# Experts that read routed rows in place, with a second product in four row tiles

## The chip, the cores and the metric

The kernel runs on one core of a Trainium2 chip. The metric is the device time of one execution in microseconds (us), the median of several runs.

## The reference, cut to what matters

The block has two halves: a gated causal cross attention (16 blocks of 128 rows, 256 wide, 16 heads), and a mixture of 32 experts, each with 4 sets. The second half is what the change works on:

```python
grouped = x.reshape(B, g, t, d)                      # groups of t = 32 rows
logits = jnp.einsum('bgtd,des->bgtes', grouped, controller) + tie
perm = (logits == jnp.max(logits, axis=-3, keepdims=True)).astype(x.dtype)
dispatched = jnp.einsum('bgtd,bgtes->bgesd', grouped, perm)
inner = jax.nn.relu(jnp.einsum('bgesd,desf->bgesf', dispatched, f1) + bias)
intermediate = jnp.einsum('bgesf,esfd->bgesd', inner, f2)
out = jnp.einsum('bgesd,bgtes->bgtd', intermediate, perm)
```

In each of 64 groups every (expert, set) slot, 128 in all, picks one row of 32; the row goes through a small network (256 to 32, relu, 32 to 256) and is added back to the row it came from.

## The kernel before, in words

Everything is float32; E = 256 is held as KH = 2 halves of 128 on the partitions. The engines run separate programs joined by semaphores; their order is written out by hand, with loops (`Fori`) whose bodies are unrolled by 2, 4 or 8. The names: PE multiplies matrices, DVE and ACT are the vector and the scalar engine, POOL is the third elementwise engine, SP issues loads and stores in the order of its program.

The start: SP issues the context tiles `cT` of blocks 0 and 1, the rows `xs`, the controller `ctrl_sb` (L211), then RING = 8 blocks of expert weights `wx` (L213, 256.5 KB each: both matrices and the bias), then in a loop the further context tiles (L220). ACT turns each context tile into its high part in `context_high` (L660), for block 2 right after the first four exponentials of block 0 (L688, L694).

Attention runs block by block over four chunks of four heads (`scores`, `weigh_v`, `transpose_p`, `softmax`, `attend`), then routing (`route`, L504 on PE): logits, a one-hot choice `pc` of a row for each slot, its transpose, and a product (L528) that gives the chosen rows. ACT (L670), for the last two blocks DVE too (L1031), keeps them in `routed[P, KH, GROUPS, SLOTS]`, one copy of 128x512 for each half of a block.

The experts: for each expert DVE first copies its four slots of all 64 groups from `routed` to a packed tile `xe` (L1038, `stage`, three experts ahead). PE multiplies `f1` of each set by it (`expert_in`, L548: 8 matmuls in four column tiles of 32, one for each set, out to a bank). DVE adds the bias and takes relu set by set (`hidden`, L1052: four instructions of 32x64) into the diagonal blocks of `hb`, whose other blocks POOL zeroed at the start. PE multiplies `f2` by this block-diagonal tile (`expert_out`, L556: 2 matmuls of full depth 128 with 256 moving columns). ACT writes the result back over the same slots of `routed` (L765). `expert_in` of the next expert stands ahead of `expert_out` of this one. SP loads expert e + 8 once expert e is through (L226).

The last stage, for each of 16 blocks: DVE packs four groups from `routed` into `yg` (L1074), PE transposes them (`transpose_y`, L596, 8 transposes), ACT copies the result to `ys` (L775, two copies), POOL copies the block's choice `permT` to `pg` (L313), PE multiplies both (`combine`, L611, four column tiles), DVE adds it to `xs` (L1078) and SP stores it (L231). The transposes of block b + 1 stand ahead of `combine` of block b.

In the trace each f32 matmul is two instructions, each with its own weight load; a transpose is one.

Of the kernel before, what the change touches and what calls it, by code (L numbers as in the profile page):

```python
# [17 lines left out]
F32 = mybir.dt.float32  # L18
# [7 lines left out]
P = 128  # L26
# [14 lines left out]
RING = 8  # L41
XR = 4
# [7 lines left out]
def build(nc, x, ctxT, wattn, gbo, ctrl, wexp, constf, out):  # L50
    with ExitStack() as ctx:
# [6 lines left out]
        bank = [ctx.enter_context(nc.psum_tensor(f"bank{i}", [P, 512], F32)) for i in range(8)]  # L58
# [18 lines left out]
        tg = sb("tg", [P, 2])  # L77
        ctrl_sb = sb("ctrl_sb", [P, KH, SLOTS])
# [32 lines left out]
        routed = sb("routed", [P, KH, GROUPS, SLOTS])  # L111
        wx = sb("wx", [P, RING, KH * P + E + 1])
        xe = sb("xe", [P, XR, KH, NS, GROUPS])
        hb = sb("hb", [P, 2, NS, GROUPS])
        yg = sb("yg", [P, 2, KH, NG, SLOTS])
        pg = sb("pg", [P, 2, P])
# [6 lines left out]
        small_loaded = sem("small_loaded")  # L123
        gates_loaded = sem("gates_loaded")
# [57 lines left out]
        xe_ready = sem("xe_ready")  # L182
        h_done = sem("h_done")
        h_ready = sem("h_ready")
        e_done = sem("e_done")
        e_kept = sem("e_kept")

        permT_kept = sem("permT_kept")
        yg_ready = sem("yg_ready")
        pg_ready = sem("pg_ready")  # L190
# [13 lines left out]
        def _(sp):  # L204
# [6 lines left out]
            sp.dma_start(ctrl_sb[:, :, :], ctrl).then_inc(small_loaded, 16)  # L211
# [9 lines left out]
            with sp.Fori(1, NE // RING) as i:  # L221
                e = i * RING
                for r in range(RING):

                    sp.wait_ge(e_done, e + (r - RING + 1))
                    sp.dma_start(wx[:, r], wexp[e + r]).then_inc(wx_loaded[r], 16)  # L226
# [10 lines left out]
        def _(pool):  # L237
            pool.memset(qz[:, :, :, :, :], 0.0).then_inc(zeroed, 1)
            pool.memset(va[:, :, :, :], 0.0).then_inc(zeroed, 1)
            pool.memset(hb[:, :, :, :], 0.0).then_inc(zeroed, 1)  # L240
# [30 lines left out]
            for k in range(2):  # L271
                split_context(k, k + 1)
            pool.wait_ge(bo_ready, 1)
# [30 lines left out]

            pool.wait_ge(permT_kept, NB)
            for k in range(2):
                pool.tensor_copy(pg[:, k, :], permT[:, k, :]).then_inc(pg_ready, 1)
            with pool.Fori(1, NB // 2) as i:
                b = i * 2
                for k in range(2):  # L310

                    pool.wait_ge(c_done, b + (k - 1))
                    pool.tensor_copy(pg[:, k, :], permT[:, b + k, :]).then_inc(pg_ready, 1)  # L313
# [3 lines left out]
        def _(pe):  # L317
# [76 lines left out]
            def attend(b, k, first=False, second=False, third=False, final=False):  # L394


                for c in range(NC):
# [45 lines left out]
                    if final and c == 3:  # L443
                        pe.wait_ge(small_loaded, 16)
# [97 lines left out]
            BH, BE = bank[0:2], bank[2:4]  # L542

            def expert_in(r):
                k = r % 2
                for s in range(NS):
                    for h in range(KH):
                        last = pe.matmul(BH[k][s * F:(s + 1) * F, 0:GROUPS],  # L548
                                         wx[:, r, h * P + s * F:h * P + (s + 1) * F], xe[:, r % XR, h, s, :],
                                         start=(h == 0), stop=(h == KH - 1), tile_position=(0, s * F))  # L550
                last.then_inc(h_done, 1)

            def expert_out(r):
                k = r % 2
                for h in range(KH):
                    last = pe.matmul(BE[k][:, h * E:(h + 1) * E], wx[:, r, KH * P + h * P:KH * P + (h + 1) * P],  # L556
                                     hb[:, k].rearrange("p s g -> p (s g)"), start=True, stop=True)
                last.then_inc(e_done, 1)

            def expert(e, r, loads):  # L560

                if loads is not None:
                    pe.wait_ge(wx_loaded[(r + 1) % RING], loads)
                    pe.wait_ge(xe_ready, e + 2)
                    if r > 0 or not isinstance(e, int):

                        pe.wait_ge(h_ready, e)
                    expert_in((r + 1) % RING)
                pe.wait_ge(h_ready, e + 1)
                if not isinstance(e, int) or e >= 2:  # L570

                    pe.wait_ge(e_kept, e - 1)
                expert_out(r)
# [4 lines left out]
            pe.wait_ge(wx_loaded[0], 16)  # L578
            pe.wait_ge(xe_ready, 1)
            expert_in(0)  # L580
            for e in range(2):
                expert(e, e, 16)
            with pe.Fori(0, NE // RING - 1) as i:
                for r in range(2, RING + 2):
                    expert(i * RING + r, r % RING, i * 16 + 16 * (1 + (r + 1) // RING))
            for r in range(2, RING):
                expert(NE - RING + r, r, 16 * (NE // RING) if r < RING - 1 else None)
# [4 lines left out]
            def transpose_y(k):  # L592
# [6 lines left out]
            def combine(b, k, early=False, final=False):  # L599

                if not final:
                    pe.wait_ge(yg_ready, b + 2)
                    if not isinstance(b, int) or b >= 1:
                        pe.wait_ge(ys_ready, b)
                    transpose_y(1 - k)
                pe.wait_ge(ys_ready, b + 1)
                pe.wait_ge(pg_ready, b + 1)
                if not early:
                    pe.wait_ge(yo_ready, b - 1)
                for g in range(NG):  # L610
                    last = pe.matmul(BC[k][g * T:(g + 1) * T, 0:E], pg[:, k, g * T:(g + 1) * T],  # L611
# [3 lines left out]
            pe.wait_ge(e_kept, NE)  # L615
            pe.wait_ge(yg_ready, 1)
            transpose_y(0)
            combine(0, 0, early=True)
            combine(1, 1, early=True)
            with pe.Fori(1, (NB - 2) // 2) as i:  # L620
                b = i * 2
                for k in range(2):
                    combine(b + k, k)
            combine(NB - 2, 0)
            combine(NB - 1, 1, final=True)
# [3 lines left out]
        def _(act):  # L629
# [37 lines left out]
            def keep_d(b, k, halves=KH):  # L667
                act.wait_ge(d_done, b + 1)
                for h in range(halves):
                    last = act.activation(routed[:, h, bass.ds(b * NG, NG), :],  # L670
                                          bank[5 - 2 * k + h][:, :].rearrange("p (g s) -> p g s", g=NG), ACT.Copy)
# [89 lines left out]
            with act.Fori(0, NE // 2) as i:  # L761
                e = i * 2
                for k in range(2):
                    act.wait_ge(e_done, e + (k + 1))
                    act.activation(routed[:, :, :, bass.ds((e + k) * NS, NS)],  # L765
                                   bank[2 + k][:, :].rearrange("p (h s g) -> p h g s", h=KH, s=NS), ACT.Copy)\
                        .then_inc(e_kept, 1)


            with act.Fori(0, NB // 2) as i:  # L770
                b = i * 2
# [378 lines left out]
```

## Time and profile before

| what | value |
|---|---|
| median of 3 runs | 329.9 us (329.48 to 330.55) |
| profiled execution, first to last instruction | 326.0 us |
| PE busy | 286.1 us (88%) |
| DVE busy | 264.4 us (81%) |
| ACT busy | 196.3 us (60%) |
| POOL busy | 112.3 us (34%) |
| PE granted clock over the span | 0.990 of full |

A time of an instruction group is given in us, a mean duration in ns. PEld is PE's weight load, which overlaps its matmuls. An engine's busy share says how full it is, not whether the end waits for it.

### The profile page before, as it was taken

How to read it: one execution, taken by the hardware profiler on the slowest of the kernel's cores; microseconds unless marked ns; L12 is line 12 of the kernel's file. 1: busy time of each engine (PE TensorE's matmuls, PEld its weight loads, DVE VectorE, ACT ScalarE, POOL GpSimd, SP SyncE). 2: the span in 40 equal slices, each digit the busy share in tenths (PEclk: the TensorE clock that was granted, in tenths of full speed). 3: DMA queues.
4: the chain of work that ended last, by engine and by line, in shares of the span. 5: the costliest groups of instructions: out<-in, count | busy, mean ns of one | idle time of the engine just before them, and what ended most of it. 6: DMA issues, size and time to landing. Idle time of an engine off the chain costs nothing.

```text
span 326.0 us, 9319 instructions
## 1 busy us (share of the span) xinstructions
PE 286.1 (88%) x3088; PEld 209.9 (64%) x3088; DVE 264.4 (81%) x675; ACT 196.3 (60%) x738; POOL 112.3 (34%) x156
## 2 busy tenths in 40 slices
PE   2299899999999999999999968899687777787995
PEld 2247577777787778787877647677365444555662
DVE  1968988978787878787879868999899999985663
ACT  2057777777777777777777863687232233225663
POOL 4124554455445644563455561455000000000110
PEclk9999999999999999999999997999899999999999
DMA  7940000000000000000000000000045454300222
GB/s 208 369 182 4 18 18 0 19 18 17 0 16 16 16 0 16 16 16 0 16 0 0 2 2 0 1 2 0 0 131 135 151 136 129 97 2 16 80 80 82
DMA packets 12355, 16.41 MB, mean 50 GB/s; under 512 B 1200, under 2 KB 7728, under 8 KB 12336
## 3 DMA queue, kind: packets, MB, share of 16 engines
q1 hardware_dynamic: 11472, 14.83, 14.9%
q10 hardware_dynamic: 864, 1.33, 1.3%
q8 instruction: 11, 0.18, 0.3%
q14 instruction: 8, 0.07, 0.1%
HBM read 14.06 MB, written 2.10 MB: 50 GB/s over the span
## 4 chain that ended last, share of the span: by engine, by line
PE 57%; DVE 26%; issue 11%; DMA 2%; ACT 2%; POOL 1%; DVEq 0%; ACTq 0%; SPq 0%; POOLq 0%
PE bank L359 10%; PE bank L352 9%; PE bank L368 9%; DVE hb L1052 8%; PE bank L328 8%; PE bank L338 7%; PE bank L596 5%; PE bank L348 3%; PE bank L611 3%; DVE xe L1038 2%; DMA xs<-in_x_dram 2%; DVE nmax L912 2%; PE bank L528 1%; DVE permb L901 1%; DVE stats L824 1%
## 5 line engine op out<-in xcount | busy, mean ns | idle before, releaser
L688 ACT ACTIVATE pr<-bank,nmax 128x128 f32<-128x128 f32 x256 | 90.3, 368 | 25.1 <-PE bank L359 18.5
L263 POOL TENSOR_TENSOR pr<-pr,rsum 128x512 f32<-128x512 f32 x64 | 66.6, 1040 | 89.4 <-DVE rsum L861 89.1
L352 PE MATMUL bank<-kd,qz 128*32 128x128 f32 (+3 forms) x512 | 66.7, 437 | 0.0
L368 PE MATMUL bank<-pT,va 128*32 128x128 f32 x512 | 62.3, 274 | 1.7 <-ACT pT L653 1.3
L912 DVE TENSOR_REDUCE nmax<-bank 128x4 f32<-128x512 f32 x64 | 44.0, 687 | 19.9 <-PE bank L352 18.6
L688 ACT ACTIVATION_READ_ACCUMULATOR pr<-bank,nmax 128x1 f32 x256 | 52.9, 207 | 0.0
L368 PEld LDWEIGHTS bank<-pT,va 128*32 128x32 f32 x512 | 38.6, 110 | 17.1 <-ACT pT L653 2.5
L556 PE MATMUL bank<-hb,wx 128*128 128x256 f32 x128 | 37.5, 417 | 12.5 <-DVE hb L1052 12.5
L765 ACT ACTIVATE routed<-bank 128x512 f32 x32 | 19.1, 597 | 45.0 <-PE bank L556 45.0
L359 PE MATMUL bank<-cf,pr 128*128 128x128 f32 x256 | 42.0, 286 | 1.6 <-POOL pr L263 1.5
L1052 DVE TENSOR_SCALAR hb<-bank,wx 32x64 f32<-32x64 f32 x128 | 36.0, 281 | 2.9 <-PE bank L548 0.6
L359 PEld LDWEIGHTS bank<-cf,pr 128*128 128x128 f32 x256 | 26.8, 140 | 15.1 <-issue 11.5
L556 PEld LDWEIGHTS bank<-hb,wx 128*128 128x128 f32 x128 | 22.4, 195 | 19.6 <-DVE hb L1052 15.9
L313 POOL COPY pg<-permT 128x128 f32 x14 | 4.1, 294 | 87.5 <-PE bank L611 87.5
L653 ACT ACTIVATE pT<-bank 128x512 f32<-128x512 f32 x32 | 19.1, 598 | 18.0 <-PE bank L359 18.0
L328 PE MATMUL bank<-cT,w 128*128 128x128 f32 x128 | 18.1, 286 | 6.2 <-DMA w<-in_wattn_dram 5.6
L874 DVE COPY pT<-bank 128x512 f32<-128x512 f32 x32 | 22.1, 689 | 1.7
L843 DVE TENSOR_SCALAR xn<-xs,mv,rs 128x256 f32 (+1 forms) x32 | 23.4, 732 | 0.0
L1038 DVE COPY xe<-routed 128x512 f32 (+1 forms) x32 | 22.4, 710 | 1.0
L775 ACT ACTIVATE ys<-bank 128x512 f32<-128x512 f32 x32 | 17.3, 596 | 9.4 <-PE bank L596 9.4
L670 ACT ACTIVATE routed<-bank 128x512 f32 (+1 forms) x30 | 16.4, 595 | 8.9 <-PE bank L528 8.7
L848 DVE TENSOR_TENSOR kd<-bank,cf 128x512 f32<-128x512 f32 x32 | 21.4, 672 | 0.4 <-PE bank L328 0.4
(91 smaller groups left out, 538.8 us busy)
## 6 DMA issues: line engine op xcount, KB each, us to landing
wx<-in_wexp_dram SPq DMA_DIRECT2D x32, 256.5 KB, 2.7
cT<-in_ctxT_dram SPq DMA_DIRECT2D x16, 128.0 KB, 2.0
xs<-in_x_dram SPq DMA_DIRECT2D x4, 512.0 KB, 10.3
out_dram<-xs SPq DMA_DIRECT2D x16, 128.0 KB, 1.7
w<-in_wattn_dram ACTq DMA_DIRECT2D x4, 256.0 KB, 7.7
cf<-in_constf_dram ACTq DMA_DIRECT2D x1, 148.0 KB, 5.9
gb<-in_gbo_dram ACTq DMA_DIRECT2D x1, 129.0 KB, 7.6
ctrl_sb<-in_ctrl_dram SPq DMA_DIRECT2D x1, 128.0 KB, 10.7
```

The lines of the kernel that those rows point to most:

```text
L263: pool.tensor_tensor(pr[:, c % 2], pr[:, c % 2], rsum[:, c * HC:(c + 1) * HC, None].to_broadcast([P, HC, P]), ALU.mult)\
L328: last = pe.matmul(dst[:, o * P:(o + 1) * P], weight[:, i, o * P:(o + 1) * P], src[:, i, :], start=(i == 0), stop=(i == KH - 1))
L338: last = pe.matmul(dst[:, 0:E], stationary, moving, start=(q == 0), stop=(q == len(parts) - 1))
L352: last = pe.matmul(bs[r, :, 0:(j + 1) * DP], qz[:, k, c // 2, c % 2, r], kd[:, k, c // 2, :, 0:(j + 1) * DP], start=False, stop=True, tile ...
L359: last = pe.transpose(BT[:, j * P:(j + 1) * P], pr[:, c % 2, j, :], ident)
L368: last = pe.matmul(BO[k][j * DP:(j + 1) * DP, o:o + P], va[:, k, c * HC + j, D * (1 - odd):][:, 0:DP], pT[:, c % 2, j * P:(j + 1) * P], st ...
L556: last = pe.matmul(BE[k][:, h * E:(h + 1) * E], wx[:, r, KH * P + h * P:KH * P + (h + 1) * P], hb[:, k].rearrange("p s g -> p (s g)"), sta ...
L688: last = act.activation(pr[:, c % 2, j, :], BS[c % 2][:, j * P:(j + 1) * P], ACT.Exp, bias=nmax[:, c * HC + j:c * HC + j + 1], accum_out=p ...
L843: dve.tensor_scalar(xn[:, k, :], xs[:, b, :], mv[:, b, 0:1], rs[:, bass.ds(b, 1)], ALU.subtract, ALU.mult).then_inc(ready, 1)
L912: dve.tensor_reduce(nmax[:, c * HC:(c + 1) * HC], BS[c % 2][:, :].rearrange("p (j t) -> p j t", j=HC), AX_X, ALU.max, negate=True).then_in ...
L1038: dve.tensor_copy(xe[:, k].rearrange("p h s g -> p h g s"), routed[:, :, :, bass.ds(e * NS, NS)]).then_inc(xe_ready, 1)
L1052: last = dve.tensor_scalar(hb[q, k, s, :], bank[k][q, 0:GROUPS], wx[q, r, KH * P + E:], 0.0, ALU.add, ALU.max)
```

## The change: what it does

- `routed` is laid out as [P, KH, SLOTS, GROUPS], and slots are ordered set by set, so the 64 groups of one slot are contiguous. The controller is loaded into `ctrl_in` and POOL reorders its columns into `ctrl_sb`, after a wait for the load, ahead of its first `bias_x`. Routing's copies (ACT and DVE) write four groups (16 bytes) for each of 128 slots.
- `xe`, `yg`, `pg` and the zeroing of `hb` are gone. `expert_in` and the last stage's PE instructions read `routed` and `permT` directly; a transpose reads its 128 slots 256 bytes apart.
- One relu for each expert, 128x64: ACT does the even experts (with Relu and a bias column), DVE the odd ones. `hb` is [P, 4, GROUPS], and the first product of an expert goes to bank e % 4.
- The second product is made for a pair of experts: 16 matmuls, each for one expert, half and set, in row tile s (32 rows of weights, 128 columns, 64 moving columns), to bank 4 + s. ACT copies banks 4 and 5, DVE banks 6 and 7 back to `routed`.
- RING is 16. SP issues 16 expert blocks at the start, the other 16 as pairs are done.
- In the last stage ACT makes one copy over two banks for each block, and DVE only the sum.
- The experts and the last stage are written out without loops.

```diff
-RING = 8
+RING = 16
+HR = 4
+PAIRS = NE // 2
...
-            sp.dma_start(ctrl_sb[:, :, :], ctrl).then_inc(small_loaded, 16)
+            sp.dma_start(ctrl_in[:, :, :], ctrl).then_inc(small_loaded, 16)
...
+            for e in range(RING, NE):
...
+                sp.wait_ge(e_done, (e - RING) // 2 + 1)
+                sp.dma_start(wx[:, e - RING], wexp[e]).then_inc(wx_loaded[e - RING], 16)
...
+            pool.wait_ge(small_loaded, 16)
+            pool.tensor_copy(ctrl_sb[:, :, :].rearrange("p h (s e) -> p h s e", s=NS),
+                             ctrl_in[:, :, :].rearrange("p h (e s) -> p h s e", s=NS)).then_inc(ctrl_ready, 1)
...
+            def expert_in(e):
...
+                for h in range(KH):
+                    for s in range(NS):
+                        last = pe.matmul(bank[e % HR][s * F:(s + 1) * F, 0:GROUPS],
+                                         wx[:, e % RING, h * P + s * F:h * P + (s + 1) * F],
+                                         routed[:, h, s * NE + e, :], start=(h == 0), stop=(h == KH - 1),
+                                         tile_position=(0, s * F), skip_group_check=True)
+                last.then_inc(h_done, 1)
+
+            def expert_out(p):
+
+                pe.wait_ge(h_ready_act, p + 1)
+                pe.wait_ge(h_ready_dve, p + 1)
+                if p > 0:
+                    pe.wait_ge(y_kept_act, p)
+                    pe.wait_ge(y_kept_dve, p)
+                for e in (2 * p, 2 * p + 1):
                     for h in range(KH):
...
+                        for s in range(NS):
+                            o = h * 2 * GROUPS + (e % 2) * GROUPS
+                            last = pe.matmul(bank[4 + s][:, o:o + GROUPS],
+                                             wx[s * F:(s + 1) * F, e % RING, KH * P + h * P:KH * P + (h + 1) * P],
+                                             hb[s * F:(s + 1) * F, e % HR, :], start=True, stop=True,
+                                             tile_position=(s * F, 0), skip_group_check=True)
                 last.then_inc(e_done, 1)
...
+            for p in range(PAIRS):
+                if p < PAIRS - 1:
+                    expert_in(2 * p + 2)
+                    expert_in(2 * p + 3)
+                expert_out(p)
...
-                        last = pe.transpose(BY2[k][g // 2][:, o:o + P], yg[:, k, h, g, :], ident)
+                        last = pe.transpose(BY2[k][g // 2][:, o:o + P], routed[:, h, :, b * NG + g], ident)
...
+            def hidden(e):
+
+                act.wait_ge(h_done, e + 1)
+                if e >= HR:
+                    act.wait_ge(e_done, (e - HR) // 2 + 1)
+                act.activation(hb[:, e % HR, :], bank[e % HR][:, 0:GROUPS], ACT.Relu,
+                               bias=wx[:, e % RING, KH * P + E:]).then_inc(h_ready_act, 1)
+
+            def keep_y(p):
+                act.wait_ge(e_done, p + 1)
+                act.activation(by_set[:, 0:2, :, 2 * p * GROUPS:2 * (p + 1) * GROUPS],
+                               banks[:, 4:6, 0:4 * GROUPS].rearrange("p s (h x) -> p s h x", h=KH), ACT.Copy)\
+                    .then_inc(y_kept_act, 1)
```

## Rows read from the trace of the kernel before

**Rows 1.** The page: span, busy time of each engine, the instruction queue's packets.
```profile
span 326.0 us, 9319 instructions
...
PE 286.1 (88%) x3088; PEld 209.9 (64%) x3088; DVE 264.4 (81%) x675; ACT 196.3 (60%) x738; POOL 112.3 (34%) x156
...
q8 instruction: 11, 0.18, 0.3%
```

**Rows 2.** Window of the experts: stretch, length, busy us (x) of PE, PEld, DVE, ACT, POOL, clock, DMA.
```profile
240.00:284.00 44.00, 34.50 (x460) 22.05 (x452) 41.56 (x114) 13.73 (x23) 0.00 (x0) 1.00 0.48 137
```

**Rows 3.** Timeline of one expert's round: start, length, engine, line, operation.
```profile
248.68 1.17 DVE L1052 TENSOR_SCALAR hb<-bank,wx 32x64 f32<-32x64 f32 x4
...
249.04 0.45 PE L548 MATMUL bank<-xe,wx 128*32 128x64 f32 x16
...
249.88 0.71 DVE L1038 COPY xe<-routed 128x512 f32 x1
...
249.90 1.13 PE L556 MATMUL bank<-hb,wx 128*128 128x256 f32 x4 [0.41 <-DVE hb L1052]
250.62 1.17 DVE L1052 TENSOR_SCALAR hb<-bank,wx 32x64 f32<-32x64 f32 x4
...
251.16 0.60 ACT L765 ACTIVATE routed<-bank 128x512 f32 x1 [1.32 <-PE bank L556]
```

**Rows 4.** Timeline at the experts' two ends.
```profile
230.81 0.69 DVE L1031 COPY routed<-bank 128x512 f32<-128x512 f32 x1 [0.29 <-PE bank L528]
...
232.44 0.96 PE L548 MATMUL bank<-xe,wx 128*32 128x64 f32 x32 [1.67 <-DVE xe L1038]
...
296.35 0.41 PE L596 MATMUL bank<-cf,yg 128*128 128x128 f32 x2 [1.60 <-DVE yg L1074]
```

**Rows 5.** Timeline of one round of the last stage.
```profile
316.69 0.86 PEld L596 LDWEIGHTS bank<-cf,yg 128*128 128x128 f32 x8 [0.41 <-issue]
316.69 1.09 PE L596 MATMUL bank<-cf,yg 128*128 128x128 f32 x8
...
317.71 0.16 PEld L611 LDWEIGHTS bank<-ys,pg 128*32 128x32 f32 x8 [0.17 <-issue]
317.71 0.64 PE L611 MATMUL bank<-ys,pg 128*32 128x256 f32 x8
...
318.28 1.09 PE L596 MATMUL bank<-cf,yg 128*128 128x128 f32 x8
```

**Rows 6.** Line 548: durations of one instruction, min/median/max ns, first and last start.
```profile
L548 PE MATMUL bank<-xe,wx x512: 216/219/317, 232.4 to 292.0; 128*32 128x64 f32 x171
```

**Rows 7.** Windows around the change from routing to the experts.
```profile
232.00:234.00 2.00, 0.91 (x32) 0.65 (x32) 1.96 (x7) 0.00 (x0) 0.00 (x0) 1.00 0.00 0
234.00:236.00 2.00, 1.70 (x4) 1.06 (x4) 1.89 (x6) 0.00 (x0) 0.00 (x0) 0.62 0.00 0
236.00:238.00 2.00, 2.00 (x20) 1.47 (x20) 1.89 (x6) 0.60 (x1) 0.00 (x0) 0.53 0.24 27
```

**Rows 8.** The start: issues, POOL, ACT's context copy; landing of L213, L220, L211.
```profile
4.84 3.59 SPq L211 DMA_DIRECT2D ctrl_sb<-in_ctrl_dram  x1
...
13.18 0.35 SPq L220 DMA_DIRECT2D cT<-in_ctxT_dram  x1
...
16.23 0.75 POOL L255 TENSOR_TENSOR xs<-xs,gb 128x256 f32<-128x256 f32 x1 [6.45 <-DVE gb L964]
...
21.87 0.43 ACT L660 ACTIVATE cTh<-cT 128x256 fp32r<-128x256 f32 x1
...
L213 SPq DMA_DIRECT2D wx<-in_wexp_dram x8: 432/432/872, 8.5 to 12.3; - x8
...
DMA to landing us min/median/max: 7.7/8.4/8.6
...
DMA to landing us min/median/max: 1.9/2.0/8.1
...
DMA to landing us min/median/max: 10.7/10.7/10.7
```

More of the change, by code:

```diff
@@ L56, in sem @@
             return ctx.enter_context(nc.semaphore(name))
-        bank = [ctx.enter_context(nc.psum_tensor(f"bank{i}", [P, 512], F32)) for i in range(8)]
+        banks = ctx.enter_context(nc.psum_tensor("banks", [P, 8, 512], F32))
+        bank = [banks[:, i, :] for i in range(8)]
         cf = sb("cf", [P, P + HC + P + NG + DP])
@@ L303, in _ @@
                     split_rows(NB - 1, 3)
[L305 to L313, printed above, removed]
         @block.tensor
@@ L553, in expert_out @@
[L553 to L557, printed above, removed]
-                last.then_inc(e_done, 1)
[L560 to L573, printed above, removed]
+            def expert_in(e):
+                pe.wait_ge(wx_loaded[e % RING], 16 * (e // RING + 1))
+                if e >= HR:
+                    if e % 2 == 0:
+                        pe.wait_ge(h_ready_act, (e - HR) // 2 + 1)
+                    else:
+                        pe.wait_ge(h_ready_dve, (e - HR) // 2 + 1)
+                for h in range(KH):
[5 more added lines that the diff above has]
+                last.then_inc(h_done, 1)
@@ L576, in _ @@
             pe.wait_ge(d_kept, NB)
             pe.wait_ge(d_kept_dve, 2)
-            pe.wait_ge(wx_loaded[0], 16)
-            pe.wait_ge(xe_ready, 1)
-            expert_in(0)
             for e in range(2):
[L582 to L587, printed above, removed]
+                expert_in(e)
@@ L1041, in hidden @@
-            def hidden(e, r, loads, early=False, left=NE):
-                k = r % 2
-                if not early:
-                    dve.wait_ge(e_done, e - 1)
-                dve.wait_ge(wx_loaded[r], loads)
-                dve.wait_ge(h_done, e + 1)
-                for s in range(NS):
-                    q = slice(s * F, (s + 1) * F)
-                    last = dve.tensor_scalar(hb[q, k, s, :], bank[k][q, 0:GROUPS], wx[q, r, KH * P + E:],
-                                             0.0, ALU.add, ALU.max)
-                last.then_inc(h_ready, 1)
-                if left > XR - 1:
-                    stage(e + XR - 1, (r + XR - 1) % XR)
@@ L1073, in stage_y, with hidden @@
[L1073 to L1076 removed]
+            def hidden(e):
+                dve.wait_ge(h_done, e + 1)
+                if e >= HR:
+                    dve.wait_ge(e_done, (e - HR) // 2 + 1)
+                dve.tensor_scalar(hb[:, e % HR, :], bank[e % HR][:, 0:GROUPS], wx[:, e % RING, KH * P + E:],
+                                  0.0, ALU.add, ALU.max).then_inc(h_ready_dve, 1)
@@ new lines, in keep_y @@
+            def keep_y(p):
+                dve.wait_ge(e_done, p + 1)
+                dve.tensor_copy(by_set[:, 2:4, :, 2 * p * GROUPS:2 * (p + 1) * GROUPS],
+                                banks[:, 6:8, 0:4 * GROUPS].rearrange("p s (h x) -> p s h x", h=KH))\
+                    .then_inc(y_kept_dve, 1)
+            hidden(1)
+            for p in range(PAIRS):
+                if p < PAIRS - 1:
+                    hidden(2 * p + 3)
+                keep_y(p)
+            for b in range(NB):
@@ L1093, in _ @@
-            dve.wait_ge(yT_done, NB - 2)
-            stage_y(NB - 1, 1)
-            for b in range(NB - 4, NB):
-                finish(b, b % 2)
 def constants():
```

139 lines of the change are left out of this document (44 added, 95 removed).

## The prediction, made before the change was run

> **What bounds the kernel now.** I read the page first: span 326.0 us, PE busy 88% of it, DVE 81% [rows 1]. The busy times by stage come next [rows 2]: from 240 to 284 us the experts, where DVE is busy 41.56 of 44 us and PE only 34.50. Attention and routing stand before, the last stage behind. The change works on the experts and the last stage, so I read one expert in order of time [rows 3]. The four relu pieces take DVE from 248.68 to 249.85, the staging copy for a later expert follows at once until 250.59, and the next relu starts at 250.62: a round of 1.94 us, all of it DVE. PE's first product (16 instructions, 0.45 us) and second (1.13 us) fit inside, and the second waits 0.41 us for relu. ACT's copy of 0.60 us is hidden. So 32 experts cost about 62 us, and the whole stretch from PE's first expert matmul at 232.44 to the first transpose at 296.35 is 63.9 us [rows 4]. In the last stage a round is 1.59 us (316.69 to 318.28), PE busy in all of it: 8 transposes, then 8 combining instructions [rows 5].
>
> The profiled execution is 326.0 us long from first to last instruction; the median of the runs is 329.9, so 3.9 us lie around the span. I sum against 326.0 and add 3.9.
>
> **Entry to the experts.** The staging copies go, PE reads the routed rows where they lie. Routing's last results are there at 231.50, PE starts at 232.44, after a wait for the staged tile [rows 4]. About 0.85 us saved.
>
> **Relu and copies.** Each relu becomes one instruction of 128x64 instead of four of 32x64; four take 1.17 us, one 0.28, by columns and not by partitions. ACT does the even experts: its 128x512 takes 0.60 us, so 64 columns take less, I say 0.25. The results of a pair are four banks of 256 columns; ACT and DVE each copy 512 columns, 0.60 us (the ACT row) and 0.69 us (the DVE copy from PSUM) [rows 3, 4]. Per pair DVE has 0.97 us and ACT 0.85, instead of twice 1.88 and twice 0.60. Neither bounds.
>
> **Second product.** It becomes 16 matmuls per pair, each 32 rows deep, 128 weight columns, 64 moving columns; in the trace every f32 matmul is two instructions, so 32 with 32 weight loads. No row of this kernel has tiles by rows; tiles by columns it has. The first product runs 16 such instructions in 0.45 us of which 0.22 is one's own length [rows 3, 6]: (0.45 - 0.22)/15 = 15 ns from one to the next. The combine does 8 weight loads of 32 columns in 0.16 us, so loads of four tiles overlap too [rows 5]. A load of 128 columns is longer: the transposes do 8 such in 0.86 us, 0.11 us each, with PE's passes beside them at the same pace [rows 5]; I take 0.11 us. If the four row tiles work side by side, each has 8 loads and 8 matmuls per pair, the load the longer one: 7 x 0.11 + 0.22 = 0.99 us from the first start to the last end. Bounds: matmul-paced as in the first product, 31 x 0.015 + 0.22 = 0.69 us; with no overlap of loads, 31 x 0.11 + 0.22 = 3.63 us. I take 0.99, by the nearest rows, which are all of four tiles.
>
> **The round of a pair.** The four result banks are single, so the chain is: second product of p, copy of p, second product of p+1. After a product's last end, 249.90 + 1.13 = 251.03, ACT starts at 251.16, 0.13 us later; DVE's copy is 0.69; and PE follows a DVE result within 0.05 us (249.85 to 249.90) [rows 3]. Round: 0.99 + 0.13 + 0.69 + 0.05 = 1.86 us. The first products of the next pair, 2 x 0.45 us with their mode changes, lie beside the copy and its end (PE alone: 0.88 for the stream, 0.5 for the first products, and 0.16 for each of two changes of tile shape, as between the last load of a transpose, 317.55, and the first of a combine, 317.71: about 1.7 [rows 5]); they are the cover, and if they took longer than 0.87 us the excess would be paid 16 times. Relu of the next pair fits under the product. Start-up: two first products, one relu, 1.3 us. Sum: 1.3 + 16 x 1.86 = 31.1 us for the 63.9 of before: 32.8 saved.
>
> **The clock** was granted at 0.62 and 0.53 of full from 234 to 238 us, that is the lower level (1.2 GHz) for about 3.4 us, after PE had been busy for only 0.91 of the 2 us before [rows 7]. Then DVE bound and it cost little; now PE's weight loads would be in the chain. I add 1.0 us, with 0 and 2 as ends.
>
> **Last stage.** The transposes read routed with 256 bytes between elements instead of a packed copy; in a transpose this is the stationary operand, the one loaded as weights. The loads now take 0.86 us for 8 beside PE's 1.09 [rows 5]; that difference is all the cover there is. No row has a PE operand so read. The nearest are ACT's and DVE's strided copies: the expert copy to 16-byte pieces 0.60 us, the staging read of 16-byte pieces 0.71 against 0.69 for a plain copy [rows 3, 4]. I take no cost; the other end is a load of twice 0.11 us: 8 x 0.11 x 16 = 14.1 us. DVE's packing, POOL's copies and the register arithmetic of the loop are hidden now, so what goes there gains nothing, except the first packing, which the 63.9 us already hold. ACT's one copy of 1024 columns instead of two is hidden under PE. The round stays 1.59 us.
>
> The Trainium skill (Advanced Engine Details and Errata, Memory Cachelines) says SBUF is read in 16-byte lines and that an access pattern with each element in another line is penalized. The ACT and DVE rows don't show it, but they have four floats per line; by the page every one of the 128 transposes would load slower, which is the rival of 316 below.
>
> **The longer ring.** Sixteen instead of eight expert blocks are queued by SP before the context tile of block 2. In the trace the eight are issued from 8.5 us, land 7.7 us after the first issue and 8.6 after the last (12.3), so from 16.2 to 20.9 us, one every 0.67 us [rows 8]. The context tile, issued right behind them at 13.18, lands 8.1 us later, at 21.3, where later ones take 2.0: it stands behind them in the queue. ACT reads it at 21.87, just in time [rows 8]. With eight more it lands at 21.3 + 8 x 0.67 = 26.7, and ACT sits in the middle of its softmax: 4.8 us. Behind that wait are all the exponentials of block 0 and so everything. PE and DVE can work ahead by some half a microsecond that counts; PE then idles some 3 us and may get the half clock for a while, as after routing. Sum: +5.0 us, ends 3.5 and 7. The new reordering of the controller by POOL waits for a load that lands at 4.84 + 10.7 = 15.5 us (4.84 is its issue, 10.7 its time to landing [rows 8]); POOL's next work was at 16.23 [rows 8]: no cost, at most 0.5. Of the expert loads, the second sixteen need 16 x 0.67 = 10.7 us and have seven rounds of 1.86 before the first is due: hidden. Routing's results are now written in 16-byte pieces, as ACT does in the expert stage at the same 0.60 us: no cost.
>
> **Sum.** 326.0 - 0.85 - 32.8 + 1.0 + 5.0 = 298.4 us; with 3.9 around it, 302 us.
>
> **Rivals.**
> 1. Slower: weight loads of row tiles don't overlap. Round 3.63 + 0.87 = 4.50 us, 16 of them 72.0 instead of 29.8: 344 us. It decides from 0.08 us per load on: the 28 us saved are 1.75 per pair, and (0.99 + 1.75 - 0.22)/31 = 0.08. For it: a load of 128 columns is seen every 0.11 us at best [rows 5], and none in row tiles. Against: loads of column tiles overlap fully.
> 2. Still faster than before, but less: the strided weight load takes double (14.1 us, 316 us); or loads overlap in twos (31 x 0.055 + 0.22 = 1.93, +15 us, 317 us); or the unrolled code, about 128 PE instructions per pair, is fetched too slowly. The instruction queue brought 0.18 MB in 11 packets over the whole kernel [rows 1]; were one needed for every two pairs and each uncovered by some 1.8 us (a guess below the 2.0 us of a small load [rows 8]), eight would be 14 us. The expert stage before shows no such stall, but it loops.
> 3. Better: row tiles paced as the first product, 0.30 us less per pair, 297 us; or the context tile comes in time after all, 5 us less, also 297. Both: 293.
>
> The Trainium skill (TensorE: Matmul & The Clock Gate, Part 3) gives 3.07 times for four row tiles with 512 columns, for tiles side by side, and says weight loads overlap when the row group differs; that is the forecast's case, but no run here shows row tiles yet.
>
> **How the numbers follow.** Forecast 302 us, chance 0.57 (296 to 308 with the bounds of the clock and the stall). Rival 1 0.16, rival 2 0.19, rival 3 0.06; that ring and experts cancel near no change 0.02. The range 294 to 319 takes in rivals 2 and 3 and leaves rival 1 out. A measurement tells about 0.3%, 1 us. Faster 0.81, same 0.02, slower 0.17.
>
> **What would show it.** The experts stage 31 us from first matmul to first transpose, rounds of 1.86 us and PE waiting for the copies; 32 instructions of the second product in about 1 us; ACT idle some 4.8 us before its context copy near 27 us, released by the DMA; last-stage rounds of 1.59 us. Wrong if rounds exceed 2.3 us, if transposes start more than 0.12 us apart, or if ACT's wait is absent.

## The result, and the profile after

| | before | after |
|---|---|---|
| median of the runs | 329.69 us (327.87 to 330.55) | 320.15 us (317.53 to 322.06) |
| profiled execution, first to last instruction | 326.0 us | 318.2 us |
| PE granted clock over the span | 0.990 | 0.930 |

The ratio of after to before is 0.9714, 95% interval 0.9657 to 0.9771. The sign was right, the size was not: 302 us was forecast with a range up to 319, and 18 of the 28 us expected did not come. Before and after were timed side by side. Within one changed kernel a slower run is one with a lower mean clock (after: 317.53 us at 0.938, 322.06 us at 0.919). The page of the changed kernel answers [rows 1]; its last line is the granted clock in 40 slices of 8 us:

```profile
span 318.2 us, 9488 instructions
...
PE 286.0 (90%) x3472; PEld 223.0 (70%) x3472; DVE 212.5 (67%) x531; ACT 190.8 (60%) x722; POOL 107.8 (34%) x140
...
PEclk9999999999999999999999997799999755559999
```

DVE is no longer the fullest engine, as intended. The slice of 7 and the four of 5 from 247 us on are the experts. The two 7s from 191 us on lie in attention and routing, which the change leaves nearly alone; such a dip there comes and goes from one profiled execution to the next. Next the windows there (stretch, length, busy us of PE, PEld, DVE, ACT and POOL with their counts, granted clock, DMA share, GB/s):

```profile
240.00:244.00 4.00, 3.53 (x134) 3.14 (x128) 1.80 (x5) 1.54 (x5) 0.00 (x0) 1.00 0.64 199
...
246.00:248.00 2.00, 0.55 (x24) 0.48 (x24) 0.38 (x2) 0.43 (x2) 0.00 (x0) 1.00 0.85 251
248.00:250.00 2.00, 1.67 (x68) 1.47 (x68) 1.11 (x3) 0.80 (x2) 0.00 (x0) 0.96 0.55 202
...
250.00:282.00 32.00, 30.43 (x640) 27.39 (x640) 10.06 (x20) 9.30 (x20) 0.00 (x0) 0.50 0.22 69
...
288.00:290.00 2.00, 2.00 (x19) 1.47 (x18) 0.48 (x1) 1.06 (x1) 0.00 (x0) 1.00 0.19 66
```

Against [rows 2], DVE is at 1.80 of 4 us instead of 94%. But from 250 to 282 us PE runs at 0.50 of its clock (1.2 instead of 2.4 GHz), although it is busy 30.43 of the 32 us. A round at the full level and one at half, from the timeline (start, length, engine, line, operation, idle before it and what ended that); L562 is the second product, L545 the first, L756 and L1042 the copies, L751 and L1037 the relus:

```profile
242.42 1.12 PE L562 MATMUL banks<-hb,wx 32*128 32x64 f32 x32
243.47 0.49 PEld L545 LDWEIGHTS banks<-routed,wx 128*32 128x32 f32 x32
243.47 0.65 PE L545 MATMUL banks<-routed,wx 128*32 128x64 f32 x32
243.60 0.60 ACT L756 ACTIVATE routed<-banks 128x512 f32<-128x512 f32 x1 [1.23 <-PE banks L562]
243.60 0.69 DVE L1042 COPY routed<-banks 128x512 f32<-128x512 f32 x1 [0.99 <-PE banks L562]
244.09 0.31 ACT L751 ACTIVATE hb<-banks,wx 128x64 f32<-128x64 f32 x1
244.21 0.27 DVE L1037 TENSOR_SCALAR hb<-banks,wx 128x64 f32<-128x64 f32 x1
...
244.45 0.79 PE L562 MATMUL banks<-hb,wx 32*128 32x64 f32 x20 [0.33 <-ACT hb L751]
...
258.90 1.99 PE L562 MATMUL banks<-hb,wx 32*128 32x64 f32 x32
...
260.81 1.08 PE L545 MATMUL banks<-routed,wx 128*32 128x64 f32 x32
...
261.83 0.49 PE L562 MATMUL banks<-hb,wx 32*128 32x64 f32 x4
```

The first round is 244.45 - 242.42 = 2.03 us and is the chain that the prediction named: product 1.12, ended at 243.54, 0.06 to the copy, DVE's copy 0.69, 0.16 to PE. The profile names ACT's relu as what ended PE's 0.33 us, but by the code `expert_out(p)` needs the copies of pair p - 1 and the relus of its own pair, done a round earlier; this relu is for the pair after. The last thing it needed was DVE's copy, which ended at 244.29. The second round, 261.83 - 258.90 = 2.93 us, is PE alone: everything it does takes longer and nothing is waited for. Eleven rounds run at half clock, from 249.85 to 282.19; only in the last two does PE wait, 0.92 and 0.85 us for copies.

The start, where [rows 8] had ACT's context copy at 21.87, and PE's idle time behind it:

```profile
27.09 0.42 ACT L645 ACTIVATE cTh<-cT 128x256 fp32r<-128x256 f32 x1 [4.42 <-DMA cT<-in_ctxT_dram]
...
28.96 0.24 PE L340 MATMUL banks<-cb 128*32 128x128 bf16 x4 [2.46 <-ACT pr L673]
```

The gap in PE's instructions after the fourth pair (there is one), and the change to the last stage with its first transposes at half clock:

```profile
247.45 0.43 PE L545 MATMUL banks<-routed,wx 128*32 128x64 f32 x16 [1.52 <-issue]
...
282.19 3.69 PE L590 MATMUL banks<-cf,routed 128*128 128x128 f32 x16 [0.85 <-ACT routed L756]
```

One round of the last stage, answering [rows 5]: 1.95 us instead of 1.59; the eight weight loads take 1.26 instead of 0.86.

```profile
308.25 1.26 PEld L590 LDWEIGHTS banks<-cf,routed 128*128 128x128 f32 x8 [0.41 <-issue]
308.26 1.45 PE L590 MATMUL banks<-cf,routed 128*128 128x128 f32 x8
...
309.63 0.64 PE L599 MATMUL banks<-ys,permT 128*32 128x256 f32 x8
...
310.20 1.45 PE L590 MATMUL banks<-cf,routed 128*128 128x128 f32 x8
```

The account by stage, in us. PE's first expert matmul: 232.44 [rows 4] to 237.22, +4.8. Experts to the first transpose: 63.9 to 282.19 - 237.22 = 45.0, -18.9. Last stage to the end: 29.65 to 36.0, +6.4. Sum -7.7, and the spans differ by 7.8.

Theory: the shortfall is half clock in the experts (about 10 us), the strided weight load (about 5) and small terms. The main rival for the clock: the gap of 1.52 us ahead of the fall took it, and without the gap it would hold.

### The profile page after: what moved, and what is told of

It reads as the page before. It is cut to its first block, busy times and chain, and to the rows that moved or that the text cites. A ratio compares the mean times of both kernels' runs of the same rounds, so it can differ in the third digit from the quotient of the medians.

```text
span 318.2 us, 9488 instructions
## 1 busy us (share of the span) xinstructions
PE 286.0 (90%) x3472; PEld 223.0 (70%) x3472; DVE 212.5 (67%) x531; ACT 190.8 (60%) x722; POOL 107.8 (34%) x140
## 4 chain that ended last, share of the span: by engine, by line
PE 69%; DVE 13%; SPq 5%; issue 5%; DMA 3%; ACT 3%; POOL 1%; DVEq 0%; ACTq 0%; POOLq 0%
PE banks L351 10%; PE banks L344 9%; PE banks L360 9%; PE banks L562 8%; PE banks L590 7%; PE banks L320 7%; PE banks L330 7%; PE banks L545 4%; DMA cT<-in_ctxT_dram 3%; PE banks L599 3%; PE banks L340 3%; SPq L214 2%; DVE nmax L908 2%; DVE permb L897 2%; PE banks L520 1%
## 5 line engine op out<-in xcount | busy, mean ns | idle before, releaser
L673 ACT ACTIVATE pr<-banks,nmax 128x128 f32<-128x128 f32 x256 | 90.5, 369 | 24.0 <-PE banks L351 17.3
L344 PE MATMUL banks<-kd,qz 128*32 128x128 f32 (+3 forms) x512 | 66.9, 437 | 0.0
L360 PE MATMUL banks<-pT,va 128*32 128x128 f32 x512 | 62.0, 276 | 1.7 <-ACT pT L638 1.3
L908 DVE TENSOR_REDUCE nmax<-banks 128x4 f32<-128x512 f32 x64 | 44.0, 687 | 19.5 <-PE banks L344 18.2
L673 ACT ACTIVATION_READ_ACCUMULATOR pr<-banks,nmax 128x1 f32 x256 | 53.2, 208 | 0.0
L360 PEld LDWEIGHTS banks<-pT,va 128*32 128x32 f32 x512 | 38.3, 110 | 17.5 <-DVE pT L870 2.6
L351 PE MATMUL banks<-cf,pr 128*128 128x128 f32 x256 | 42.4, 289 | 1.6 <-POOL pr L261 1.5
L351 PEld LDWEIGHTS banks<-cf,pr 128*128 128x128 f32 x256 | 27.1, 141 | 15.4 <-issue 11.5
L562 PE MATMUL banks<-hb,wx 32*128 32x64 f32 x512 | 27.4, 377 | 2.1 <-ACT hb L751 1.0
L562 PEld LDWEIGHTS banks<-hb,wx 32*128 32x128 f32 x512 | 24.9, 280 | 4.5 <-issue 2.6
L756 ACT ACTIVATE routed<-banks 128x512 f32<-128x512 f32 x16 | 9.6, 598 | 30.0 <-PE banks L562 30.0
L1042 DVE COPY routed<-banks 128x512 f32<-128x512 f32 x16 | 11.1, 692 | 23.8 <-PE banks L562 23.8
## 6 DMA issues: line engine op xcount, KB each, us to landing
xs<-in_x_dram SPq DMA_DIRECT2D x4, 512.0 KB, 10.7
```

Source lines behind the costliest of these rows:

```text
L344: last = pe.matmul(bs[r, :, 0:(j + 1) * DP], qz[:, k, c // 2, c % 2, r], kd[:, k, c // 2, :, 0:(j + 1) * DP], start=False, stop=True, tile ...
L351: last = pe.transpose(BT[:, j * P:(j + 1) * P], pr[:, c % 2, j, :], ident)
L360: last = pe.matmul(BO[k][j * DP:(j + 1) * DP, o:o + P], va[:, k, c * HC + j, D * (1 - odd):][:, 0:DP], pT[:, c % 2, j * P:(j + 1) * P], st ...
L562: last = pe.matmul(bank[4 + s][:, o:o + GROUPS], wx[s * F:(s + 1) * F, e % RING, KH * P + h * P:KH * P + (h + 1) * P], hb[s * F:(s + 1) * ...
L673: last = act.activation(pr[:, c % 2, j, :], BS[c % 2][:, j * P:(j + 1) * P], ACT.Exp, bias=nmax[:, c * HC + j:c * HC + j + 1], accum_out=p ...
L908: dve.tensor_reduce(nmax[:, c * HC:(c + 1) * HC], BS[c % 2][:, :].rearrange("p (j t) -> p j t", j=HC), AX_X, ALU.max, negate=True).then_in ...
```

## The experiments

Each stands against a kernel before timed beside it on the same chip; ratios are to that. Where two changed kernels are compared ("less than after"), their medians are from different sessions, in which the kernel before took 328.3 to 329.69 us; worked out from the ratios, such a difference can be up to 1 us larger or smaller. Words like "the clock falls in the experts" are read from one profiled execution of each kernel; of the other runs only the time and the mean clock are known.

**The context tiles ahead of the second eight expert blocks.**

```diff
-            for r in range(RING):
+            for r in range(8):
                 sp.dma_start(wx[:, r], wexp[r]).then_inc(wx_loaded[r], 16)
...
+            for k in range(2):
...
+                sp.dma_start(cT[:, k], ctxT[2 + k]).then_inc(ctx_loaded[k], 16)
+            for r in range(8, RING):
+                sp.dma_start(wx[:, r], wexp[r]).then_inc(wx_loaded[r], 16)
```

> The changed kernel with one thing moved: SP issues the context tiles of blocks 2 and 3 after eight expert blocks, and the other eight expert blocks behind them. Theory: the 4.4 us that ACT waits before its third context copy go, and the time falls by 4 to 5 us from 320 to about 315.5. Rival: the wait only hid other work of the first blocks, or the later expert blocks now disturb the attention: less than 2 us.

Measured 315.66 us (311.76 to 316.19), 0.9566 [0.9496, 0.9637]: 4.5 less than after (by the ratios 4.9). The stall is paid in full and is what the prediction said. The clock falls all the same, in the profiled run at 242 us; the fastest run, 311.76 us, has a mean clock of 0.950 where the other three have 0.929.

**Packing in the last stage put back**, on DVE, into space of `wx` that is free by then.

```diff
+                dve.tensor_copy(yg[b % 2], routed[:, :, :, b * NG:(b + 1) * NG].rearrange("p h s g -> p h g s"))\
+                    .then_inc(yg_ready, 1)
...
-                        last = pe.transpose(BY2[k][g // 2][:, o:o + P], routed[:, h, :, b * NG + g], ident)
+                        last = pe.transpose(BY2[k][g // 2][:, o:o + P], yg[k][:, h, g, :], ident)
```

> The changed kernel, but DVE again packs each block's slots for the last stage (as before the change), so that the transposes load contiguous columns. Theory: the strided weight load paces the transposes (0.147 us each against 0.11); rounds of the last stage fall from 1.94 to 1.59 us, 16 of them 5.6 us, less 0.7 us for the first packing: about 5 us faster, 315. Rival: the round is longer for another reason (ACT's single copy of 1024 columns, or the code without loops): rounds stay at 1.9 and the time rises by 0.7.

Measured 315.52 us (314.74 to 316.3), 0.9591 [0.9555, 0.9627]: 4.6 less than after (by the ratios 4.0). The rounds of the last stage are 1.59 us again (starts at 289.16 and 290.75), so the strided weight load is shown as the cause of the longer ones. One packing now takes DVE 1.36 us. It is not all hidden: the first transposes wait 2.30 us for it, where in after they wait 0.85 for a copy, and the last rounds are 1.63 to 1.69 us, since packing and sum together fill DVE.

**No second half of the expert loads.** The result is that of the wrong weights for experts 16 to 31; all other work is the same, without DMA traffic beside it.

```diff
-            for e in range(RING, NE):
-
-                sp.wait_ge(e_done, (e - RING) // 2 + 1)
-                sp.dma_start(wx[:, e - RING], wexp[e]).then_inc(wx_loaded[e - RING], 16)
```

> The changed kernel without the second sixteen expert loads; experts 16 to 31 use the weights of 0 to 15, so this part of the result is left wrong. It asks why the PE clock is at the lower level from 250 us. Theory A (one gap takes it): the 1.5 us in which PE stands still at 246 us, with the expert loads on the DMA engines, is a slow fetch of code; without the loads the gap goes and the clock stays up, the experts take 16 rounds of 2.03 us, some 10 us less. Theory B (the work itself is too thin): the clock falls at about the same place although the gap is gone, and the time falls by 1.5 us only.

Two runs, 308.8 us at a mean clock of 0.978 and 319.5 at 0.930. In the profiled one (the first) the gap, at the same instruction (four products and half of the next pair's first ones done), is 0.15 us, and by the windows the clock falls about 16 us later than in after, at 266 us:

```profile
243.56 0.43 PE L541 MATMUL banks<-routed,wx 128*32 128x64 f32 x16
244.14 0.43 PE L541 MATMUL banks<-routed,wx 128*32 128x64 f32 x16
```

```profile
256.00:264.00 8.00, 6.80 (x252) 5.89 (x249) 3.61 (x8) 3.30 (x8) 0.00 (x0) 1.00 0.02 4
264.00:266.00 2.00, 1.39 (x49) 1.16 (x50) 0.90 (x2) 0.80 (x2) 0.00 (x0) 1.00 0.01 4
266.00:268.00 2.00, 1.20 (x28) 1.01 (x24) 0.69 (x1) 0.60 (x1) 0.00 (x0) 0.55 0.05 12
```

So the gap is larger with the expert loads beside it, and a gap of that size is not needed for the fall: from 244 to 266 us PE is never idle for more than 0.34 us at a stretch (the usual wait of each round, and three short gaps of 0.18, 0.25 and 0.31 us that no row explains, the last ending at 264.33), and the clock falls. Neither expectation holds as written: the gap nearly went, and the clock fell all the same, but 16 us later. The two runs are 10.7 us apart, and the faster is the one with the late fall.

**Four full-array matmuls a pair as filling**, 128x128 weights, 256 columns, results thrown away, ahead of the second product.

```diff
+                for _ in range(4):
+                    pe.matmul(bank[2 * p % HR][:, E:2 * E], rh[:, 0, 0:P],
+                              permb[:, 0, 0:2, :].rearrange("p g s -> p (g s)"), start=True, stop=True,
+                              skip_group_check=True)
```

> The changed kernel with four extra full-array matmuls (f32r, 256 columns, into a part of a bank that nobody reads) in each pair, placed where PE would wait for the copies; all loads stay. Theory B (thin work): the extra work holds the clock at the upper level, rounds are 2.03 to 2.2 us instead of 2.93, and the time falls by 7 to 10 us to about 311. Theory A (the gap): the gap is still there, the clock falls as before, and the extra work costs 0 to 0.4 us a round, so the time is 320 to 327.

Four runs in two groups: 311.1 and 315.27 us at clocks of 0.987 and 0.978, 332.62 and 333.23 at 0.915 and 0.917, slower than before. So four sometimes hold it. The profiled execution (one of the first group) speaks against the rival: it has the gap, and the clock stays up through the experts, so that the products after it take their full-level 1.12 us. The slower pair has no trace.

```profile
248.72 0.65 PE L545 MATMUL banks<-routed,wx 128*32 128x64 f32 x32 [1.24 <-issue]
...
249.97 1.12 PE L566 MATMUL banks<-hb,wx 32*128 32x64 f32 x32
```

**Eight of them**, the same edit with range(8).

> The changed kernel with eight instead of four extra full-array matmuls in each pair (0.9 us of them a round). Theory (thin work): with twice the full-array work the clock holds in all runs; rounds are 2.03 + 0.2 + 0.44, about 2.7 us at the upper level, and the time is 315 to 318 with little spread. Rival (a pause takes the clock whatever else is done): runs still split in two groups, some near 316 and some near 340.

Measured 318.69 us (317.02 to 320.06), 0.9686 [0.964, 0.9733], the clock of every run 0.982 to 0.999, so the clock holds as expected; the time is just above the 315 to 318 expected. PE does 1.2 us more work in each of 16 rounds, and the kernel is no slower for it than after, since the clock (and the gap, which is gone here) is worth as much. PE is never idle in the middle of the stage:

```profile
240.00:280.00 40.00, 40.00 (x1042) 35.78 (x1035) 12.62 (x29) 11.38 (x29) 0.00 (x0) 1.00 0.33 109
```

**One pause**, in the kernel without the second loads: PE waits once for a POOL memset.

```diff
+            pool.wait_ge(e_done, 5)
+            pool.memset(va[:, :, :, :], 0.0).then_inc(gap_done, 1)
...
+                if p == 5:
+                    pe.wait_ge(gap_done, 1)
```

> The kernel without the second sixteen loads (part of the result wrong, as there), in which the profile held the upper clock level until 266 us, with one pause put in: after pair 4 PE waits for a POOL memset of 1.4 us. Theory (thin work does not bring the clock back, a pause takes it): the clock falls within some 5 us of the pause, near 248 to 252 us, stays at the lower level to the end of the experts, rounds are 2.93 us from there, and the time is near the 318 to 320 of the changed kernel. Rival (only the loads or the length of thin work take it): the clock holds to 260 us or longer as without the pause, and the time is 310 or 311.

Measured 319.07 (the profiled run), 318.97 and 313.3 us (clocks 0.935, 0.934, 0.959). The trace shows the fall between 244 and 248 us, and then half clock for 35 us:

```profile
245.11 1.54 PE L562 MATMUL banks<-hb,wx 32*128 32x64 f32 x32
248.16 1.08 PE L545 MATMUL banks<-routed,wx 128*32 128x64 f32 x32 [1.50 <-POOL va L305]
```

```profile
244.00:248.00 4.00, 1.95 (x52) 1.65 (x48) 1.41 (x3) 1.15 (x3) 1.28 (x1) 0.71 0.02 4
...
252.00:280.00 28.00, 27.08 (x584) 24.52 (x576) 8.77 (x18) 7.92 (x18) 0.00 (x0) 0.50 0.01 3
```

The product just ahead of the pause already takes 1.54 us where 1.12 is the full level, so the fall began before the pause that I made, right behind the known gap, here 0.70 us. As a test of a pause the run is void. But two things stand. In all five traces of row tiles alone in which that gap is 0.70 us or more (after, the early context tiles, the packed stage, this one, and the row tiles with both repairs below) the clock falls within 2.5 us of its end; in the one with 0.15 us it holds for 20 us more. So the gap does seem to bring the fall forward, which is a coincidence of traces and no test. And row-tiled work, busy 27.08 of 28 us and without DMA traffic, doesn't bring the clock back.

**The row tiles undone**: full depth, block-diagonal `hb` as before, relu in four pieces. With it goes a second difference: the results of two pairs are buffered, so PE waits for the copies of pair p - 2 and no longer for those of p - 1. All else is as changed.

```diff
-                    pe.wait_ge(y_kept_act, p)
-                    pe.wait_ge(y_kept_dve, p)
+                if p > 1:
+                    pe.wait_ge(y_kept_act, p - 1)
+                    pe.wait_ge(y_kept_dve, p - 1)
...
+                        last = pe.matmul(bank[4 + e % 4][:, h * E:(h + 1) * E],
+                                         wx[:, e % RING, KH * P + h * P:KH * P + (h + 1) * P],
+                                         hb[:, e % HR].rearrange("p s g -> p (s g)"), start=True, stop=True)
```

> The changed kernel with the row tiles alone undone: the second product again has full depth 128 with a block-diagonal moving tile of 256 columns, relu again in four pieces for each expert (ACT and DVE share them), results of an expert in one bank, two pairs buffered. Theory (the clock follows how much of the array works): PE's round is longer, 1.7 + 0.5 + 0.3 = 2.5 us at the upper level, against 2.03 with row tiles, but the clock stays up, so that 16 rounds take 40 us instead of the 45 us of the changed kernel, and the time falls by 4 to 6 us to about 315. Rival (the clock falls because of the waits of the new order, whatever the product): it falls here too and the time rises by 5 us or more.

Measured 316.03 us (314.55 to 318.52), 0.9618 [0.9559, 0.9677], clocks 0.978 to 0.988: 4.1 less than after (by the ratios 3.2, and the two intervals overlap a little; the cleaner comparison comes below), with more work for all three engines in each round. The relu pieces lie under the product, and PE bounds the round of 2.51 us (260.66 - 258.15):

```profile
258.15 2.00 PE L561 MATMUL banks<-hb,wx 128*128 128x256 f32 x8
258.30 1.26 ACT L751 ACTIVATE hb<-banks,wx 32x64 f32<-32x64 f32 x4
258.40 1.17 DVE L1041 TENSOR_SCALAR hb<-banks,wx 32x64 f32<-32x64 f32 x4
260.08 0.65 PE L546 MATMUL banks<-routed,wx 128*32 128x64 f32 x32
...
260.66 0.70 PE L561 MATMUL banks<-hb,wx 128*128 128x256 f32 x2
```

**All three together**: block-diagonal product, early context tiles, packed last stage.

> The three repairs together on the changed kernel: full-depth block-diagonal second product, context tiles of blocks 2 and 3 ahead of the second eight expert loads, packed columns for the transposes. Theory: the gains add, as they are in three different stages: 4.4 + 4.4 + 5 us below the changed kernel, about 306. Rival: in the last stage or the experts DVE becomes the bound (relu pieces 1.17 and copies 0.69 us of a round of 2.5), and the sum is 3 us or more short.

Measured 307.74 us (307.42 to 308.24), 0.9365 [0.9343, 0.9386], every clock between 0.988 and 0.994. It beats both kernels, by 21 and by 12 us. It is 1.7 us short of the 306 expected; part of that is in the last stage, where DVE, busy 9.00 of the 9 us from 289 to 298, stretches the rounds to 1.68 us, as the rival had it. Its experts, and two starts of its last-stage rounds, 1.59 us apart:

```profile
240.00:270.00 30.00, 30.00 (x481) 23.08 (x480) 21.69 (x61) 21.78 (x61) 0.00 (x0) 1.00 0.41 125
```

```profile
278.47 1.09 PE L597 MATMUL banks<-cf,wx 128*128 128x128 f32 x8
...
280.06 1.09 PE L597 MATMUL banks<-cf,wx 128*128 128x128 f32 x8
```

**The same two repairs with the row tiles kept.**

> The row tiles of the change kept, with the context tiles issued after 8 expert blocks and the packed last stage, so only the second product differs from the kernel with the block-diagonal one (307.74). Theory (thin row-tiled work leaves the clock low once it has fallen): terms add, 320.15 - 4.5 - 4.6 = 311 us, with a spread of several us from run to run, a clock falling to half somewhere in the experts, and rounds of 2.03 us before and 2.93 us after it. Rival (the fall came from the late context tile or from the strided loads near by): the clock stays up, 16 rounds of 2.03 us, 302 to 304 us, faster than the block-diagonal kernel.

Measured 312.12 us (310.61 to 313.6), 0.9509 [0.947, 0.9548]. The terms add to within 1.1 us of the 311 worked out, the fall of the clock is not an effect of the late context tile or the strided loads, and the row tiles cost 4.4 us against the block-diagonal product (with its second buffer); here the intervals of the ratios are far apart. In the trace:

```profile
244.00:280.00 36.00, 32.78 (x653) 29.86 (x654) 13.34 (x23) 9.93 (x21) 0.00 (x0) 0.50 0.20 61
```

**And with eight matmuls of filling on top.**

> The same with eight full-array matmuls of 256 columns ahead of each pair's second product, results thrown away. Theory: clock at full level in all runs, PE busy in the whole round, as with the filling alone: 318.7 - 4.5 - 4.6 = 309.6 us, spread under 3 us; so that 308 is no worse than it and block-diagonal work is the better way of holding the clock. Rival (filling costs less beside the packed stage than alone): below 306 us.

Measured 311.92 us (310.25 to 312.25), 0.949 [0.9458, 0.9521], clocks 0.988 to 0.994. The clock is held through the experts, as expected; the time is 2.3 us above the 309.6, so at this place filling gains nothing over leaving the clock low. Of the two ways of holding the clock only the block-diagonal product pays: three quarters of its multiplications are by zeros, but its round is 2.51 us where the one with fillings is 2.77, and 16 times the difference is the 4.2 us between 311.92 and 307.74.

## Why the prediction went wrong, point by point

**The bound and the chain: right.** DVE was the bound, and it is gone. The chain product, copy, product holds as written at the full level. The round there is 2.03 us and not 1.86: the product is 1.12 instead of 0.99, and the two handovers 0.06 + 0.16 instead of 0.13 + 0.05. That is 0.17 x 16 = 2.7 us, before the clock falls.

**Row tiles side by side: right.** 32 instructions with loads in 1.12 us; rival 1 (3.63 us) is out. The Trainium skill (TensorE: Matmul & The Clock Gate, Part 3) says that row tiles run beside each other, and this trace agrees with 32 in 1.12 us.

**The clock: the step that failed.** I added 1.0 us, ends 0 and 2, by [rows 7], where the clock was low for 3.4 us after routing and came back. I took the length of that fall as the length of any. But there it came back while PE did block-diagonal products of 256 columns, the very work that the change removes. In after it stays low for 11 rounds at 2.93 instead of 2.03 us, 9.9 us. The start of the last stage is slow too: from the first transpose to the end it takes 36.0 us, against 34.4 with eight fillings, where the same code starts at the full level, so 1.6 us more. The term was 1.0 and measured 11.5. This also overturned the rate I gave to PE: at half clock PE bounds the round, not the copies.

The runs put the low clock on the thin tiles. The four kernels with much full-array work in each pair (two block-diagonal, two with eight fillings) hold 1.00 through the experts in their profiles, and their mean clock is 0.978 or more in all 17 runs. In the six with row tiles alone (after, the early context tiles, the packed last stage, the two without the second loads, the one with both repairs) the profiled execution loses it in the experts and gets it back only in the last stage. The mean alone proves less: 0.978 is also the mean of the run without the second loads, whose clock fell at 266 us.

Two other things differ between these groups, and no run separates them fully. The four that hold the clock have no gap, and in the middle of the stage (242 to 270 us) no idle time of PE at all, while PE in after, at the full level from 240 to 244 us, is busy 3.53 of 4 us. Against idle time as the cause stands the kernel before, busy 34.50 of 44 us at 1.00 [rows 2]. Against the gap stands the profile with four fillings, which has it and holds. And once the clock is low, waits don't keep it there: from 250 to 266 us PE in after is busy 16.00 of 16 us at 0.50. So that thin work doesn't bring the clock back is shown; what tips it over, and at which moment, stays open. Thin tiles without any idle time, started at the full level, were not run.

**The last stage: the other mis-sized term.** I took 0 for the strided weight load, from the rows of ACT and DVE, and 14.1 as the other end. The load of eight takes 1.26 instead of 0.86 us (one load 257 ns instead of 141), and the round is 0.35 us longer. Over the whole stage at the full level that is 34.4 against 29.65 us, 4.7 more. The 0.23 us that I called cover was none: it is the time by which the last transpose ends after the last load, and 0.19 of it is still there in after. The loads paced the transposes already, so 0.36 of the 0.40 us came through (1.45 for 1.09). "Nearest row" was the wrong guide, since those rows read four floats side by side in 16 bytes and the transposes one. The Trainium skill (Advanced Engine Details and Errata, Memory Cachelines) says that an access pattern with each element in another line is penalized; the trace agrees, at 1.26 against 0.86 us for eight loads.

**The longer ring: right.** 4.8 us forecast for the wait, 4.42 seen, 4.5 gained by undoing it. ACT's copy came at 27.09, forecast "near 27". PE idled 2.46 us and kept its clock. POOL's next work behind the reordering of the controller came at 17.08 instead of 16.23; what that costs is not separated from the wait.

**Entry: right.** PE starts 0.10 us after the last routed copy (237.12 to 237.22) and not 0.94, so 0.84 us are saved for the 0.85 forecast. The start of the experts still moved by 4.78 us in place of 4.15. The 0.6 us lie ahead of it, in attention and routing, whose clock differs between profiled executions: from 190 to 231 us it is 0.96 before, 0.92 in after and 1.00 in the packed kernel, and in seven kernels with the late context tile the experts start anywhere from 235.28 to 238.51.

**Code fetch, a guess of rival 2:** one gap of 1.52 us, not eight. It is at the same instruction of the loop-free code in all six kernels with row tiles alone, 1.25 to 1.52 us with the expert loads beside it and 0.15 and 0.70 without; with four fillings it is 1.24, and with eight, or with the block-diagonal product, PE shows none. The instruction queue brought 17 packets instead of the 11 of [rows 1]. That the gap is a fetch behind the expert loads fits these, but was not tested by itself.

**Around the span:** of my 3.9 us only 1.7 to 2.2 lie around it in any run whose span is known (after: 319.98 for 318.2); the rest was, as far as these numbers tell, that the profiled execution of before was shorter than the timed ones.

The sum mended: 298.4 + 0.6 (ahead of the experts) + 2.7 (round) + 9.9 + 1.6 - 1.0 (clock) + 1.3 (gap, beyond the round it falls in) + 4.7 (last stage) = 318.2, and the span is 318.2. Most terms are read from this same trace, so that they add up is bookkeeping and no further proof. The rivals had the strided load, the stall and the gap, and none had the clock. A rival "the clock stays low for the whole stage" could have been worked out from rows at hand: PE alone needs 1.7 us a round by the prediction, so at most 3.4 at half clock against the round of 1.86, an estimate of up to 25 us for 16 rounds. The signs that I named did show it: rounds above 2.3 us and transposes more than 0.12 us apart.

## What to carry to other kernels

A busy PE is not a fast PE: when wide matmuls are cut into thin tiles, price the stage at both clock levels, and take the levels from stretches that do the same kind of work. Before queueing more prefetch, look for the small transfer that is issued behind it, and put it first. A layout that saves a copy can move its cost into the weight loads of PE; see first whether the loads pace PE already, since then nothing covers them.

## What the runs showed of the hardware

- PE at 0.50 of its clock for 32 us while busy 30.43 of them, on row tiles of 32x128 with 64 columns and column tiles of 128x32 with 64 columns; four wide matmuls more per pair (128x128 weights, 256 columns, one instruction each in the trace) kept it up in two runs of four, eight in all nine.
- Four row tiles side by side: 32 loads of 32x128 and 32 f32 matmul instructions of 64 columns in 1.12 us at the full level, 1.99 at half.
- A stationary operand read with 256 bytes between elements: eight loads of 128x128 in 1.26 us instead of 0.86, one in 257 ns instead of 141.
- The same time (312.12 and 311.92 us in all) with PE at half clock and thin work, and at full clock with 1.21 us more of PE work in each pair.
